# Last eight tiles of a patch-embed, FFT-mixer and routed-FFN tower: the exponential table, the first quad's gate and one product moved

## The reference

```python
h = einsum("bnf,fh->bnh", patches, W)                    # 768 -> 256
x = layernorm(h)
x_proj = x @ in_w + in_b
mod = gelu(x @ mod_w1 + mod_b1) @ mod_w2 + mod_b2        # 256 -> 1024 -> 256
modulated = x_proj * mod
y = irfft(rfft(modulated) * rfft(kernel))                # over the 196 tokens of an image
h = h + y @ out_w + out_b
x = layernorm(h)
logits = x @ router_W.T + router_b                       # 6 experts, softmax, best 2, shares made to sum to 1
hidden = x @ routed_A                                    # 6 experts x rank 16 = 96 columns
h = h + x @ base_W.T + base_b + shared(x) + (hidden * share) @ routed_B
```

## Time and profile before

| | us |
|---|---|
| median of 3 runs | 1240.4 |
| lowest, highest run | 1240.23, 1243.64 |
| the profiled execution | 1241.79 |
| its span, first to last instruction | 1240.0 |
| PE busy in the span | 1226.8 (99%) |
| DVE busy | 858.9 (69%) |
| ACT busy | 584.4 (47%) |
| POOL busy | 395.2 (32%) |
| the mean granted clock of PE | 0.999 of full speed |

### The profile page before, as it was taken

One profiled execution on the slowest core, in us unless ns is written; L12 is line 12 of the kernel. 1 busy time (PEld: TensorE's weight loads), 2 busy tenths in 40 slices (PEclk: granted clock), 3 DMA queues, 4 the chain that ended last, 5 costly groups with the idle time before them and its releaser, 6 DMA issues.

```text
span 1240.0 us, 21100 instructions
## 1 busy us (share of the span) xinstructions
PE 1226.8 (99%) x8154; PEld 1198.9 (97%) x8154; DVE 858.9 (69%) x2559; ACT 584.4 (47%) x1109; POOL 395.2 (32%) x459
## 2 busy tenths in 40 slices
PE   8999999999999999999999999999999999999998
PEld 7899999999999999999999999999999999999996
DVE  5567766667766667666677676677666677666676
ACT  6545445444444454544454444444454445443441
POOL 2532233232233232333322333322332323332220
PEclk9999999999999999999999999999999999999999
DMA  7201111101111101111101111011111011110001
GB/s 245 77 6 47 52 52 41 49 14 52 51 52 40 51 14 52 52 52 39 37 29 51 52 52 39 18 48 51 52 40 51 14 53 51 52 39 17 14 13 35
DMA packets 24414, 57.26 MB, mean 46 GB/s; under 512 B 2873, under 2 KB 19578, under 8 KB 20474
## 3 DMA queue, kind: packets, MB, share of 16 engines
q1 hardware_dynamic: 24314, 55.92, 12.9%
HBM read 43.07 MB, written 12.85 MB: 45 GB/s over the span
## 4 chain that ended last, share of the span: by engine, by line
PE 95%; DVE 1%; DMA 1%; ACT 1%; SPq 1%; issue 0%; DVEq 0%
PE rotating L1394 17%; PE rotating L1396 17%; PE rotating L1395 17%; PE rows_ps L1394 10%; PE rows_ps L1395 10%; PE rows_ps L1396 10%; PE turn L1683 4%; PE turn L1667 2%; PE turn L1446 2%; PE rows_ps L1456 2%; PE turn L1394 1%; PE turn L1395 1%; PE turn L1396 1%; PE rotating L1527 1%; DMA gelu<-dram_w 1%; DMA patches<-dram_x_first 0%
## 5 line engine op out<-in xcount | busy, mean ns | idle before, releaser
L632 ACT ACTIVATE gelu<-rotating,biases 128x392 f32<-128x392 f32 x256 | 148.8, 582 | 203.2 <-PE rotating L1396 203.1
L502 POOL TENSOR_TENSOR folded<-modulated 128x196 f32<-128x196 f32 x63 | 37.9, 602 | 557.9 <-DVE modulated L1068 557.9
L489 POOL TENSOR_TENSOR gelu_l<-gelu,gelu_h 128x784 fp32r<-128x784 f32 x62 | 117.4, 1893 | 224.1 <-DVE norm L1051 198.2
L484 POOL TENSOR_TENSOR patches_l<-patches,patches_h 128x384 fp32r<-128x384 f32 (+1 forms) x186 | 181.8, 1006 | 4.3 <-ACT patches_h L581 4.3
L1394 PE MATMUL rotating<-x_h,w_h 128*128 128x392 f32 x512 | 177.4, 347 | 0.5 <-ACT gelu L632 0.5
L1394 PE MATMUL rotating<-gelu_h,w_h 128*128 128x392 f32 x512 | 177.8, 347 | 0.0
L1395 PE MATMUL rotating<-x_l,w_h 128*128 128x392 f32 x512 | 174.6, 341 | 0.0
L1396 PE MATMUL rotating<-x_h,w_l 128*128 128x392 f32 x512 | 174.6, 341 | 0.0
L1395 PE MATMUL rotating<-gelu_l,w_h 128*128 128x392 f32 x512 | 174.4, 341 | 0.0
L1396 PE MATMUL rotating<-gelu_h,w_l 128*128 128x392 f32 x512 | 174.0, 340 | 0.0
L1394 PE MATMUL rows_ps<-tokw_h,patches_h 128*128 128x256 f32 x570 | 163.1, 286 | 2.0 <-DVE patches_l L823 2.0
(11 more groups left out here) (289 smaller groups left out, 2920.2 us busy)
## 6 DMA issues: line engine op xcount, KB each, us to landing
patches<-dram_x_rest SPq DMA_DIRECT2D x30, 1152.0 KB, 5.0
out<-h_sb SPq DMA_DIRECT2D x30, 384.0 KB, 2.5
patches<-dram_x_first SPq DMA_DIRECT2D x2, 384.0 KB, 5.7
h_sb<-dram_x_second SPq DMA_DIRECT2D x1, 768.0 KB, 7.5
patches<-dram_x_fourth SPq DMA_DIRECT2D x1, 768.0 KB, 9.6
gelu<-dram_w SPq DMA_DIRECT2D x1, 512.0 KB, 7.2
out<-h_sb SPq DMA_DIRECT2D x1, 512.0 KB, 2.9
out<-h_sb SPq DMA_DIRECT2D x2, 256.0 KB, 2.2
```

Source lines behind the costliest of these rows:

```text
L484: pool.tensor_tensor(patches_l[:, k, 0:n], patches[:, k, 0:n], patches_h[:, k, 0:n].bitcast(F32), ALU.subtract).then_inc(pool_patches_lo, 1)
L489: pool.tensor_tensor(gelu_l[:, 2 * j:2 * j + 2, :], gelu[:, 2 * j:2 * j + 2, :], gelu_h[:, 2 * j:2 * j + 2, :].bitcast(F32), ALU.subtract)\
L502: pool.tensor_tensor(folded[:, m, 0, :, 1:NF], fwd, back, ALU.add)
L632: act.activation(gelu[:, k, :], bank(g + 1, UP[k])[:, 0:GT], ACT.Gelu, bias=b1_bias[:, k:k + 1]).then_inc(act_gelu, 1)
```

## The change

- **Exponential table.** The ACT table with the exponential was loaded in `quad_exp(0)`, between the two `y_sine_half` copies. Now an exponential of four columns that nothing reads (`exp_table`) stands ahead of `last_fold_hi`, and takes the load there.
- **First quad's gate by GpSimd.** ACT copies the first quad's hidden from PSUM into SBUF (`hidden_out`, into a free half of `x_proj`), and POOL multiplies all four tiles by their shares in one instruction (`first_gated_rows`). DVE's four instructions `quad_gated_rows(0)` are gone.
- **Gate steps within the norm's chain.** The last gate links (`quad_share`: sum with epsilon, reciprocal, and the new product that spreads the shares over the experts) of the first quad stand between links of the last quad's `layer_norm_scales`. The ranks' sum is taken after the last half of y (`quad_chosen`), not ahead of it (`quad_flags`).
- **PE's list.** The inverse transform's half 0 takes its cosine products after POOL's first instruction and not its second. The first quad's last base product stands ahead of its four transposes; the last quad's stands between its first two and last two. One more `keep_clock` stands ahead of `last_quad_routes`.

The core of the diff:

```diff
+            def first_gated_rows():
+                room = quad_rooms[0]
+                pool.wait_ge(act_hidden, 1)
+                pool.wait_ge(pool_half_spec, 2)
+                pool.wait_ge(dve_gate, GATE_STEPS * (GROUPS - 2) + QUAD_GATE)
+                weight = room.wide[:, 5].rearrange("p t (e a) -> p t e a", a=1).broadcast_to([P, QUAD, EXPERTS, RANK])
+                pool.tensor_tensor(room.gated.rearrange("p t (e r) -> p t e r", r=RANK),
+                                   hidden_sb.rearrange("p t (e r) -> p t e r", r=RANK), weight, ALU.mult)\
+                    .then_inc(tile_gated, QUAD)
...
             half_spectrum()
+            first_gated_rows()
...
+            def exp_table():
+                act.activation(quad_rooms[0].small[:, 7], ident[:, 0:QUAD], ACT.Exp)
+
+            def hidden_out():
+                act.wait_ge(pe_quad_routes, 1)
+                act.activation(hidden_sb, quad_routes[0][:, :, 0:ROUTED], ACT.Copy).then_inc(act_hidden, 1)
...
             quad_normalise(0, (2, 3))
+            act.wait_ge(quad_consts, 16)
+            exp_table()
             last_fold_hi()
             first_quad_tokens_out()
+            hidden_out()
             act.wait_ge(pe_idft, DH * last + 1)
             y_sine_half(0)
             quad_exp(0)
...
                 link(dve.tensor_scalar(guess.bitcast(I32), v.bitcast(I32), -0.5, RSQRT_MAGIC, ALU.mult, ALU.add))
+                if beside:
+                    beside(0)
                 link(dve.tensor_tensor(tmp(4), guess, guess, ALU.mult))
+                if beside:
+                    beside(1)
                 link(dve.scalar_tensor_tensor(out=tmp(5), in0=tmp(4), scalar=-RSQRT_K1, in1=v, op0=ALU.mult,
                                               op1=ALU.mult))
+                if beside:
+                    beside(2)
...
                 if q == 0:
+                    dve.wait_ge(act_hidden, 1)
                     dve.wait_ge(quad_consts, 32)
...
-                quad_link(q, 5, dve.tensor_tensor(flat(1), flat(0), room.thr, ALU.is_gt))
-                quad_link(q, 6, dve.tensor_reduce(room.wide[:, 3], room.cmp[:, 1], AX_X, ALU.add))
-
-            def quad_weights_of(q):
+                quad_link(q, 5, dve.tensor_tensor(flat(1), flat(0), room.thr, ALU.is_gt), wait=False)
+
+            def quad_chosen(q):
+                dve.wait_ge(dve_gate, GATE_STEPS * (GROUPS - 2) + QUAD_GATE * q + 5)
+                quad_link(q, 6, dve.tensor_reduce(room.wide[:, 3], room.cmp[:, 1], AX_X, ALU.add))
                 dve.wait_ge(act_quad_exp, q + 1)
...
-                quad_link(q, 10, dve.scalar_tensor_tensor(out=small(4), in0=small(1), scalar=GATE_EPS, in1=small(3),
-                                                          op0=ALU.mult, op1=ALU.add))
-                quad_link(q, 11, dve.reciprocal(small(5), small(4)))
+
+            def quad_share(q, n):
+                dve.wait_ge(dve_gate, GATE_STEPS * (GROUPS - 2) + QUAD_GATE * q + 9 + n)
+                if n == 0:
+                    ins = dve.scalar_tensor_tensor(out=small(4), in0=small(1), scalar=GATE_EPS, in1=small(3),
+                                                   op0=ALU.mult, op1=ALU.add)
+                elif n == 1:
+                    ins = dve.reciprocal(small(5), small(4))
+                else:
+                    ins = dve.tensor_tensor(room.wide[:, 5], room.wide[:, 4], over_experts(small(5), QUAD), ALU.mult)
+                quad_link(q, 10 + n, ins, wait=False)
...
             quad_logits(0)
             whole_y_half(0)
-            quad_ranks(0)
+            quad_flags(0)
             whole_y_half(1)
             last_y_lo()
-            quad_weights_of(0)
+            quad_chosen(0)
             quad_mixer(1, 1, 0)
             quad_stats(1, 1, 0)
-            quad_gated_rows(0)
             quad_mixer(1, 0, 1)
             stats = quad_stats(1, 0, 1)
-            layer_norm_scales(GROUPS + 1, stats, slice(0, 2), 2)
+            layer_norm_scales(GROUPS + 1, stats, slice(0, 2), 2, beside=lambda n: quad_share(0, n))
...
-            quad_ranks(1)
-            quad_weights_of(1)
+            quad_flags(1)
+            quad_chosen(1)
+            quad_share(1, 0)
+            quad_share(1, 1)
             quad_gated_rows(1)
...
             def last_inverse_dft(m):
-                for img in range(PAIR):
-                    c = img * DIM + m * P
-                    for x in range(2):
+                for x in range(2):
+                    if m == 0:
+                        pe.wait_ge(pool_half_spec, x + 1)
+                    for img in range(PAIR):
+                        c = img * DIM + m * P
...
-            pe.wait_ge(pool_half_spec, 2)
             last_inverse_dft(0)
...
             pe.wait_ge(dve_quad_h, 3)
+            quad_base_products(0, (3,))
             for t in range(QUAD):
                 ins = quad_turn_gated(0, t)
             ins.then_inc(pe_quad_turned, 1)
-            quad_base_products(0, (3,))
...
             last_quad_turn_x2()
+            keep_clock(rows_ps[:, 1], 1)
             last_quad_routes()
-            quad_base_products(1, range(QUAD))
+            quad_base_products(1, (0, 1, 2))
             pe.wait_ge(dve_quad_h, 4)
             quad_turn_gated(1, 0)
             quad_turn_gated(1, 1).then_inc(pe_quad_turned, 1)
+            quad_base_products(1, (3,))
             quad_turn_gated(1, 2)
             quad_turn_gated(1, 3).then_inc(pe_quad_turned, 1)
```

More of the change, by code:

```diff
@@ L200, in tower_program @@
         quad_ones = quad_tokens[ROUTED:ROUTED + 1, 2 * DH * BANK:(2 * DH + 2) * BANK]
+        hidden_sb = x_proj[:, 1, 0:QUAD * ROUTED].rearrange("p (t c) -> p t c", t=QUAD)
         def quad_norm(t):
@@ L301, in tower_program @@
         dve_quad_x2 = sem("dve_quad_x2")
-        dve_tile_gated = sem("dve_tile_gated")
-        QUAD_GATE = 11
+        act_hidden = sem("act_hidden")
+        tile_gated = sem("tile_gated")
+        QUAD_GATE = 12
         pe_quad_out = sem("pe_quad_out")
@@ L894, in stats2, with layer_norm_scales @@
                 return ins
-            def layer_norm_scales(e, stats, norms, n):
+            def layer_norm_scales(e, stats, norms, n, beside=None):
                 done = [0]
@@ L1227, in quad_logits, with quad_flags @@
                                                   ALU.subtract), wait=False)
-            def quad_ranks(q):
+            def quad_flags(q):
                 room, n = quad_rooms[q], QUAD
@@ L1246, in quad_weights_of @@
                 wide = lambda c: room.wide[:, c].rearrange("p t e -> p (t e)")
+                dve.wait_ge(dve_gate, GATE_STEPS * (GROUPS - 2) + QUAD_GATE * q + 5)
+                quad_link(q, 6, dve.tensor_reduce(room.wide[:, 3], room.cmp[:, 1], AX_X, ALU.add))
                 dve.wait_ge(act_quad_exp, q + 1)
-                dve.wait_ge(dve_gate, GATE_STEPS * (GROUPS - 2) + QUAD_GATE * q + 6)
                 quad_link(q, 7, dve.scalar_tensor_tensor(out=wide(4), in0=wide(3), scalar=1.5, in1=wide(1),
@@ L1251, in quad_weights_of @@
                 quad_link(q, 8, dve.tensor_reduce(small(1), room.wide[:, 1], AX_X, ALU.add))
-                quad_link(q, 9, dve.tensor_reduce(small(3), room.wide[:, 4], AX_X, ALU.add))
-                quad_link(q, 10, dve.scalar_tensor_tensor(out=small(4), in0=small(1), scalar=GATE_EPS, in1=small(3),
-                                                          op0=ALU.mult, op1=ALU.add))
-                quad_link(q, 11, dve.reciprocal(small(5), small(4)))
+                quad_link(q, 9, dve.tensor_reduce(small(3), room.wide[:, 4], AX_X, ALU.add), wait=False)
+            def quad_share(q, n):
+                room = quad_rooms[q]
+                small = lambda c: room.small[:, c]
+                dve.wait_ge(dve_gate, GATE_STEPS * (GROUPS - 2) + QUAD_GATE * q + 9 + n)
[7 more added lines that the diff above has]
+                quad_link(q, 10 + n, ins, wait=False)
             def quad_gated_rows(q):
                 room = quad_rooms[q]
+                dve.wait_ge(dve_gate, GATE_STEPS * (GROUPS - 2) + QUAD_GATE * q + 11)
                 for t in range(QUAD):
@@ L1263, in quad_gated_rows @@
                                              in0=hidden, scalar=room.small[:, 5, t:t + 1], in1=chosen, op0=ALU.mult,
-                                             op1=ALU.mult).then_inc(dve_tile_gated, 1)
+                                             op1=ALU.mult).then_inc(tile_gated, 1)
             def last_quad_gated_out():
@@ L1627, in quad_turn_gated @@
             def quad_turn_gated(q, t):
-                pe.wait_ge(dve_tile_gated, QUAD * q + t + 1)
+                pe.wait_ge(tile_gated, QUAD * q + t + 1)
                 return pe.transpose(quad_turned[q][t // 2][:, t % 2 * TILE:(t % 2 + 1) * TILE],
```

## The result

| | before | after |
|---|---|---|
| median, us | 1240.74 | 1243.53 |
| lowest to highest, us | 1239.73 to 1243.64 | 1241.51 to 1244.96 |
| runs | 12 | 12 |
| ratio to before | 1 | 1.0023, interval 1.0016 to 1.0031 |
| profiled execution: time / span / mean granted clock | 1241.79 / 1240.0 / 0.999 | 1244.96 / 1243.2 / 0.997 |

What follows compares the result with a forecast made beforehand. It took PE, busy 99%, as waiting for DVE in the end part. Routes start +1.0, their passes -0.05 (dip included) and end -0.3 made +0.6 on the median 1240.4: 1241.0 us, range 1239.2 to 1243.0.

Steps and rivals of the forecast that it cites:

- what is late next: End part: first quad's gate through POOL ends late, so the last quad's transposes start at 1226.45, +1.0 us.
- the start behind the table load: ACT, inverse transform: the moved load makes `last_fold_hi` start 0.2 us late; PE's second-half y work starts 0.3 sooner.
- rival 4: At `last_fold_hi`: the table load brings its drain, +1.4 us, giving 1242.4; chance 0.02.
- DVE's relief: Last quad on DVE: second `quad_mixer` 1.4 us sooner, at 1219.0; norm 1.1 us sooner, at 1223.5.
- the sum: Whole kernel: routes start +1.0, their passes -0.05, the end -0.3, in all +0.6 us on the median 1240.4.
- rival 2: End part: POOL slow or dip dearest, 1241.5 to 1242.1; or median had no dip before, +1.8, 1242.2; chance 0.21.
- the size of the low stretch: PE's end part: a low-clock dip of 3.3 us, costing 0.9 to 1.7 us, taken as 1.2.
- Rival 3: End part: clock low for two stretches, first transposes into last quad's base products, +5.6 us, 1245.4; chance 0.04.
- the end: From the last quad's logits to DVE's last sum: 7.35 us becomes 7.0, a gain of 0.3.

Runs made afterwards that it cites:

- fill8: The changed kernel with eight unread `keep_clock` products ahead of the first quad's gated transposes; 1241.4 us, ratio 1.0003 to the kernel before.
- table: The kernel before with only the exponential's table load moved ahead of `last_fold_hi`; 1240.37 us, ratio 1.0001.
- before_fill: The kernel before with six unread `keep_clock` products ahead of the last quad's transposes and one behind them; 1240.33 us, ratio 0.9998.
- lastorder: The kernel before with only the last quad's fourth base product moved between its gated transposes; 1240.63 us, ratio 1.0005.
- order: The changed kernel with the last quad's transposes ahead of `quad_routed(0)` and ACT's normalised tiles ahead of its gated copy; 1243.64 us, ratio 1.0019.
- early: The changed kernel with the first quad's three last gate steps right behind `quad_chosen(0)`, not in the norm; 1239.54 us, ratio 0.9991.
- order_fill: The kernel of `order` plus eleven unread `keep_clock` products around the first quad's gated transposes; 1240.97 us, ratio 1.0001.
- pool_split: The changed kernel with POOL's product cut into two instructions of two tiles each; 1243.53 us, ratio 1.0017.
- early_oldlast: The kernel of `early` with all four of the last quad's base products ahead of its gated transposes, as before; 1239.23 us, ratio 0.9989.

## Why the prediction was right and wrong

**Right: what is late next.** The prediction put the gated transposes at 1223.35 and the last quad's at 1226.45. Carried to before's ruler, after has the first at 1205.30 + 18.13 = 1223.43, and `fill8`, at full clock, has the last quad's at 1205.30 + (1226.34 - 1204.99) = 1226.65. So the delay is +1.2 us over 1225.42, where I had +1.0. POOL took 0.88 us, not 1.01, which made up for most of a start 0.2 later. (The terms of that sum add up to 1226.47, not 1226.45; nothing hangs on it.)

**Right: the start behind the table load.** `last_fold_hi` came 0.2 late, with no drain, and rival 4 is out. The gain behind it was smaller than the 0.3 I took: 0.07 at both `quad_mixer` steps in `table` (12.75 against 12.81, 15.03 against 15.10).

**Half right: DVE's relief.** The second `quad_mixer` came 1.25 us sooner (predicted 1.4), but the norm only 0.49 (predicted 1.1). Of the missing 0.6, 0.52 is one row, L962: 0.69 us where its like take 0.17, while POOL's product ran. In after it cost nothing, because the norm was not what PE waited for.

**Wrong 1: the sum was set on the wrong base.** It credited the change with the 1.25 us that the profiled execution of before loses on its routes, and then took the result from the median, 1240.4. But the median execution of before has no low stretch: filling its waits in `before_fill` leaves the median where it was (1240.33 against 1240.25), and the profiled execution stood 1.4 us above it, which is about the 1.6 us of its low stretch. I had both numbers on the page and named this only inside rival 2, at +1.8. Against the median nothing is given back: +1.2 and the whole of the new low stretch.

**Wrong 2: the size of the low stretch.** I took a dip of the same 3.3 us and 1.2 us for it. It lasted 6.8 (before's 3.4) and cost 2.5, which the rows give piece by piece against `fill8`: `quad_routed` 3.55 against 1.80, transposes and `keep_clock` 2.14 against 1.38 (1229.36 to 1231.50; 1226.34 to 1227.72), the routes nothing, as the clock was back when they ran. That is 1.75 + 0.76 = 2.5. Rival 3 had the clock low for two such stretches, which is what came, but priced it at 5.6: it summed `quad_routed`, transposes, routes and twelve base passes. At the low level these would fill 3.5 + 1.5 + 3.2 + 5.2 = 13.4 us, twice what two stretches of 3.3 hold. With the right price, 2.5 over its own base of 1239.8, rival 3 would have stood at 1242.3 and not at 1245.4.

**Wrong 3: the end.** The new order was to gain 0.3 of 7.35 us. The forecast of what it would be, 7.0 from L, was right (7.05). What it was compared with was not: 7.35 was read in an execution whose clock was still coming back while the base products ran; at full clock it is 6.85. So the step loses 0.2 (0.3 done alone, in `lastorder`).

**The sum as it should have been:** transposes and routes +1.2, the end +0.2, both at full clock, 1.4 as the ruler says; and 2.5 for a low stretch that nearly each execution of after has, less what the median of before pays for its own, next to nothing. From the 1240.2 of before's runs without one, that gives 1240.2 + 1.4 + 2.5 = 1244.1, with 1241.6 for an execution without it. The one run of after at a mean clock of 1.000 took 1241.51, the eight at 0.997 took 1243.27 to 1244.96, and the median 1243.53 lies between. The measured +2.8 is smaller than 3.9. Two things fit this, and no run takes them apart: before's median there, 1240.74, is that of a group with half of its runs above 1241, and the four runs of after at a mean clock of 0.998 or more lie at 1241.51 to 1243.23, so not each low stretch was as long.

What stood on the page before the result: of the three runs shown, two (1240.23 and 1240.40) lie 1.6 and 1.4 us below the profiled 1241.79, about the price of its dip. That was a hint, if no proof, that they had none.

**Open:** why the same waits bring the clock down in some executions of before and not in others (40 of 106 have a mean clock below 1.000, against eleven of twelve of after); the runs show the shares, not what decides. Nor why the low stretch of `order` was 3.4 us in its trace, as before's, and that of after 6.8, behind the same 1.99 us of wait.

## What to carry to other kernels

When a step is moved off a busy engine and into a chain that has slack, follow it to its reader: here a product of 0.88 us, started 4 us later than it could be, made TensorE stand 2 us. The same three small steps put ahead of the work that they were hidden in cost 0.2 us there and gave back all of it and more (1239.54 in `early` against 1243.53). And before a term is credited from one profiled execution, ask whether the median one has it: compare its time and its mean clock with the other runs', and never subtract a dip from a median that holds none.

## What the runs showed of the hardware

**A small VectorE step waits for the end of GpSimd's instruction.** In after, L962, 128x4 with two SBUF inputs, started at 1223.64 and ended at 1224.33; POOL's product ended at 1223.43 + 0.88 = 1224.31. In `order_fill` it was the link before it, and in `pool_split` two links, ending at 1223.08 and 1223.56 where POOL's halves ended at 1223.06 and 1223.53. DVE's rows of `order_fill`, then of `pool_split`:

```profile
1222.44 0.84 POOL L524 TENSOR_TENSOR norm<-x_proj,patches 128x384 f32<-128x384 f32 x1 [9.54 <-DVE patches L1299]
```

```profile
1222.38 0.17 DVE L960 TENSOR_SCALAR ln_tmp<-ln_tmp 128x4 f32<-128x4 f32 x1
1222.46 0.84 DVE L961 TENSOR_TENSOR ln_tmp<-ln_tmp 128x4 f32<-128x4 f32 x1
1223.34 0.16 DVE L962 TENSOR_TENSOR ln_tmp<-ln_tmp 128x4 f32<-128x4 f32 x1
```

```profile
1222.72 0.36 DVE L965 TENSOR_TENSOR ln_tmp<-ln_tmp 128x4 f32<-128x4 f32 x1
1223.12 0.44 DVE L966 SCALAR_TENSOR_TENSOR ln_tmp<-ln_tmp 128x4 f32<-128x4 f32 x1
```

In `early_oldlast`, where POOL's product (1218.54 to 1219.38) runs beside the first `quad_mixer`, which reads one input from PSUM, and the statistics, which have one input, DVE's rows keep their 0.68 and 0.75 us. The Trainium skill (GPSIMD Engine Reference, "Key points") says that POOL shares its SBUF interfaces with VectorE and contends with instructions of two SBUF inputs. The trace agrees, and the sum was right to give the product no extra time for it: it was DVE that was held, not POOL. One thing the traces leave open is where the border lies: L961 in after started 0.02 us behind POOL's start and took its usual 0.16, and the same link in `order_fill`, also 0.02 us behind it, was held for 0.84.

**The table load has no second part.** In after and in `table` it starts 0.02 to 0.03 us behind the activation before it, takes 1.28 us, and the exponential starts 0.01 to 0.02 us behind its end. The further 1380 ns of the Trainium skill (ScalarE: Activation LUTs, "What ACT_TABLE_LOAD costs") are not seen.
